# The order of the row maxima, the second batch's projections and three tiles in an attention stage

## The reference, cut to what matters

```python
qkv = hidden_states @ Wqkv
q = qkv[..., :nH * d].reshape(B, S, nH, d)
k = qkv[..., nH * d:nH * d + d]
v = qkv[..., nH * d + d:]
scores = jnp.einsum('bqhd,bkd->bhqk', q, k) * scale
...
scores = jnp.where(causal[None, None], scores + alibi[None], NEG_INF)
probs = jax.nn.softmax(scores, axis=-1)
attn = jnp.einsum('bhqk,bkd->bqhd', probs, v).reshape(B, S, H)
return attn @ Wo
```

## Time and profile before

| what | value |
|---|---|
| median of three runs | 4109.71 us |
| the profiled execution | 4106.15 us |
| its span, first to last instruction | 4104.3 us |
| TensorE busy | 3618.9 us (88%) |
| VectorE busy | 2896.3 us (71%) |
| ScalarE busy | 2364.0 us (58%) |
| mean granted TensorE clock | 0.949 of full |

### The profile page before, as it was taken

One profiled execution on the slowest core, in us unless ns is written; L12 is line 12 of the kernel. 1 busy time (PEld: TensorE's weight loads), 2 busy tenths in 40 slices (PEclk: granted clock), 3 DMA queues, 4 the chain that ended last, 5 costly groups with the idle time before them and its releaser, 6 DMA issues.

```text
span 4104.3 us, 62802 instructions
## 1 busy us (share of the span) xinstructions
PE 3618.9 (88%) x21250; PEld 1809.9 (44%) x21250; DVE 2896.3 (71%) x4627; ACT 2364.0 (58%) x4071; POOL 2065.2 (50%) x1695
## 2 busy tenths in 40 slices
PE   3889998889888779999999999989999996776799
PEld 1344443223322335555555555545555553343344
DVE  4444335773576458888888888888988886657787
ACT  4533323554456556666666766766666663446665
POOL 4600000000000337787787777778777786546754
PEclk9999997998889989999999999999999997899999
DMA  3200011001100010000000000010000001013000
GB/s 104 68 6 1 1 31 17 1 1 18 36 8 4 10 37 7 25 13 14 25 1 26 13 25 13 8 31 1 25 13 20 11 1 65 1 45 80 16 11 31
DMA packets 58879, 88.92 MB, mean 22 GB/s; under 512 B 11429, under 2 KB 32440, under 8 KB 58548
## 3 DMA queue, kind: packets, MB, share of 16 engines
q1 hardware_dynamic: 57880, 84.15, 7.3%
q10 hardware_dynamic: 672, 0.59, 0.1%
HBM read 71.05 MB, written 6.85 MB: 19 GB/s over the span
## 4 chain that ended last, share of the span: by engine, by line
PE 62%; DVE 14%; issue 8%; ACT 6%; POOL 4%; DVEq 0%; ACTq 0%; DMA 0%; POOLq 0%
PE psum L257 12%; PE psum L259 12%; PE psum L258 12%; PE psum L1388 3%; DVE arena L1550 3%; PE psum L1361 2%; PE psum L2495 2%; PE psum L2483 2%; PE psum L2491 2%; PE psum L2452 2%; PE psum L1372 2%; PE psum L3148 1%; PE psum L3149 1%; DVE x L2177 1%; PE psum L2474 1%
## 5 line engine op out<-in xcount | busy, mean ns | idle before, releaser
L257 PE MATMUL psum<-xt_hi,arena 128*128 128x512 f16 (+1 forms) x1920 | 740.5, 386 | 19.4 <-ACT arena L2005 5.9
L258 PE MATMUL psum<-xt_lo,arena 128*128 128x512 f16 (+1 forms) x1920 | 738.9, 385 | 0.0
L259 PE MATMUL psum<-xt_hi,arena 128*128 128x512 f16 (+1 forms) x1920 | 737.8, 384 | 0.0
L2278 POOL TENSOR_TENSOR arena<-arena 128x1024 f16<-128x1024 f16 x256 | 515.5, 2034 | 49.5 <-DVE arena L2089 32.4
L1501 ACT ACTIVATE arena<-psum 128x512 f32<-128x512 f32 x576 | 320.2, 598 | 276.8 <-PE psum L1372 183.4
L1550 DVE TENSOR_REDUCE arena<-psum 128x1 f32<-128x512 f32 (+3 forms) x608 | 365.3, 654 | 155.3 <-PE psum L1361 154.1
L257 PE MATMUL psum<-arena 128*128 128x512 f16 (+1 forms) x1152 | 418.0, 367 | 57.8 <-DVE arena L2913 26.6
L1306 POOL TENSOR_TENSOR rs<-sd,epsc 128x1 f32<-128x1 f32 x15 | 8.1, 540 | 819.4 <-DVE sd L1598 819.4
L258 PE MATMUL psum<-arena 128*128 128x512 f16 (+1 forms) x1152 | 417.8, 367 | 0.0
L259 PE MATMUL psum<-arena 128*128 128x512 f16 (+1 forms) x1152 | 417.7, 366 | 0.0
L2283 POOL TENSOR_TENSOR arena<-arena 128x512 f16<-128x512 f16 x256 | 314.7, 1248 | 4.8 <-PE psum L2463 4.6
(11 more groups left out here) (363 smaller groups left out, 8340.8 us busy)
## 6 DMA issues: line engine op xcount, KB each, us to landing
arena<-m_wi SPq DMA_DIRECT2D x64, 320.0 KB, 3.0
arena<-m_wo SPq DMA_DIRECT2D x32, 256.0 KB, 2.6
arena<-arena SPq DMA_DIRECT2D x90, 64.0 KB
x<-L_attn_x SPq DMA_DIRECT2D x4, 1024.0 KB, 5.3
arena<-gate_wT SPq DMA_DIRECT2D x16, 224.0 KB, 2.5
arena<-up_wT SPq DMA_DIRECT2D x16, 224.0 KB, 2.5
arena<-down_wT SPq DMA_DIRECT2D x14, 256.0 KB, 2.6
out<-x SPq DMA_DIRECT2D x3, 1024.0 KB, 4.3
```

Source lines behind the costliest of these rows:

```text
L257: nc.tensor.matmul(out, lh, rh, start=start, stop=False)
L258: nc.tensor.matmul(out, lh, rl, start=False, stop=False)
L259: return nc.tensor.matmul(out, ll, rh, start=False, stop=stop)
L2278: nc.gpsimd.tensor_tensor(m4_ar[:, q], heads[q].broadcast_to([P, HG, P]), m4_le.unsqueeze(1).broadcast_to([P, HG, P]), ALU.mult).then_inc( ...
```

## The change

It changes the plan, not the work: the ring has the same 630 entries, and the same steps run on each engine.

- The second batch's tiles come in the order 0, 3, 2, 1, 4, 5, 6, 7 (before 0, 3, 1, 4, 2, 5, 6, 7).
- The ring is made as pairs of due time and entry and sorted by due time. So projections and maxima now alternate, where before one finished before the other began.
- The projections of batch 1 start a tile sooner: the first key piece at the end of tile 5, the second and the first four query pieces at 6 units' distance in tile 6, the value piece at the start of tile 7. The other four query pieces follow at one unit's distance from the last unit of tile 7 on.
- The maxima of tiles 8, 9 and 10 are spread evenly over tile 7; those of tile 11 over the next 28 units; those of tiles 12 to 15 evenly over everything up to tile 15. Per eight score units this gives nine in tile 7 (six in its last eight), four in tile 8, then 5, 6, 9, 8 in tile 9, 9, 9, 9 in tile 10, 9, 9 in tile 11, and eight or nine from there to the end of tile 14. For tile 2 they begin before tile 0, so that tile 0 has 13 and the first eight units of tile 1 have 16.
- A row step comes as soon as three further ring entries have been placed after the last maximum, or at the latest directly before its tile. In units before the tile: rows 2 to 7 come 4 (before 6), row 8 61, rows 9 and 10 40 and 41, row 11 40, row 12 19, row 13 16, row 14 6, row 15 none.
- SyncE's loads of the weight pieces are tied to a score step 7 units before the end of a tile instead of a row step, which is where they stood; the load of the next block's weights goes with row 12 instead of row 11.

```diff
--- before.py
+++ after.py
@@ -500,7 +500,7 @@
         def row_group(half, first, n):
             return slice(half * HALF + first, half * HALF + first + n)
 
-        SEQ2 = [(0, t) for t in range(TPB)] + [(1, t) for t in (0, 3, 1, 4, 2, 5, 6, 7)]
+        SEQ2 = [(0, t) for t in range(TPB)] + [(1, t) for t in (0, 3, 2, 1, 4, 5, 6, 7)]
         POS2 = {b * TPB + t: p for p, (b, t) in enumerate(SEQ2)}
         TAIL2 = (("heads0", 1), ("o0", 2), ("heads1", 4), ("o1", 5), ("turn", 7), ("turn_hi", 8), ("turn_lo", 9),
                  ("project", 11), ("y_stats", 13), ("y_sd", 14), ("y_scale", 15), ("y_norm", 16), ("add", 17), ("x_sd", 18),
@@ -511,31 +511,31 @@
 
         def plan2():
 
-            ring, when = [], []
-
-            def feed(p, at):
-                us = max_units(SEQ2[p][1])
-                for u in range(len(us)):
-                    ring.append(("max", p, u))
-                    when.append(at(u, len(us)))
-            for piece in [("qp", 0, 0, f) for f in range(KT)] + [("kp", 0, 0), ("kp", 0, 1), ("vp", 0)]:
-                ring.append(piece)
-                when.append(-1)
-            feed(0, lambda u, n: -1)
-            for p in range(NT - 1):
-                b, t = SEQ2[p]
-                start, n = first2[p] - LEAD2, units2[p]
-                if p == TPB - 1:
-                    pieces = [("kp", 1, 0), ("kp", 1, 1)] + [("qp", 1, 0, f) for f in range(KT)] + [("vp", 1)]
-                    for i, piece in enumerate(pieces):
-                        ring.append(piece)
-                        when.append(first2[p] + 3 * i)
-                    start, n = start + n - 8, 8
-                if (b, t) in ((0, 1), (1, 3)):
-                    for f in range(KT):
-                        ring.append(("qp", b, 1, f))
-                        when.append(first2[p] + 2 * f)
-                feed(p + 1, lambda u, m: start + (u + 1) * n / m)
+            ring = []
+
+            def feed(units, start, n):
+                for i, unit in enumerate(units):
+                    ring.append((max(0, start + (i + 1) * n / len(units)), unit))
+
+            of_tile = lambda p: [("max", p, u) for u in range(len(max_units(SEQ2[p][1])))]
+            for piece in [("qp", 0, 0, f) for f in range(KT)] + [("kp", 0, 0), ("kp", 0, 1), ("vp", 0)] + of_tile(0):
+                ring.append((-1, piece))
+            for f in range(KT):
+                ring.append((first2[1] + 2 * f, ("qp", 0, 1, f)))
+            for p in range(TPB - 1):
+                feed(of_tile(p + 1), first2[p] - LEAD2, units2[p])
+            for i, piece in enumerate([("kp", 1, 0), ("kp", 1, 1)] + [("qp", 1, 0, f) for f in range(KT)]):
+                ring.append((first2[TPB - 2] + 6 * i, piece))
+            last = TPB - 1
+            ring.append((first2[last] + 3, ("vp", 1)))
+            feed(of_tile(last + 1) + of_tile(last + 2) + of_tile(last + 3), first2[last] - LEAD2, units2[last])
+            for f in range(KT):
+                ring.append((first2[last + 1] + f, ("qp", 1, 1, f)))
+            feed(of_tile(last + 4), first2[last + 1] - LEAD2, 4 * LEAD2)
+            far = [unit for p in range(last + 5, NT) for unit in of_tile(p)]
+            feed(far, first2[last + 1] + 3 * LEAD2, first2[NT - 1] - first2[last + 1] - 4 * LEAD2)
+            ring.sort(key=lambda entry: entry[0])
+            when, ring = [at for at, _ in ring], [unit for _, unit in ring]
             for r in range(len(ring) - 2, -1, -1):
                 if ring[r][0] == "max":
                     when[r] = min(when[r], when[r + 1] - 1 / 1.6 if ring[r + 1][0] == "max" else when[r])
@@ -569,7 +569,10 @@
                     while r < len(RING2) and (WHEN2[r] <= now or RING2[r] == ("max", p, RING2[r][-1])):
                         steps.append(("ring", r))
                         r += 1
-                    while rows < NT and DONE2[rows] < r and (rows <= p or now >= first2[p + 1] - LEAD2 + 1):
+                        if rows < NT and DONE2[rows] + 3 < r:
+                            steps.append(("row", rows))
+                            rows += 1
+                    if rows < NT and rows <= p:
                         steps.append(("row", rows))
                         rows += 1
                     if i == 0:
@@ -1267,12 +1270,13 @@
                         held.append(p)
                     elif piece[0] == "qp" and piece[3] == KT - 1:
                         q_rows(sp, p, piece[2], range(8) if piece[1] else range(6))
+                elif what == "score" and p + 1 >= EARLY4 and u[0] == units2[p] - LEAD2:
+                    if p + 1 < NT:
+                        if p + 1 > EARLY4:
+                            sp.wait_ge(m4_wlo, p + 1 - EARLY4 + 2)
+                        sp_piece(sp, p + 1 - EARLY4)
                 elif what == "row":
-                    if p >= EARLY4:
-                        if p > EARLY4:
-                            sp.wait_ge(m4_wlo, p - EARLY4 + 2)
-                        sp_piece(sp, p - EARLY4)
-                    if p == 11:
+                    if p == 12:
                         sp.wait_ge(a2_md, AT2["qp", 1, 1, KT - 1] + 3)
                         sp.wait_ge(a2_dma, 16 * 2 * QDMA)
                         sp.dma_start(s3_raw, A["L1_ffn_sign"].rearrange("(k p) n -> p k n", p=P)).then_inc(s3_in, 16)
```

## The result

The kernel before took 4110.86 us (median of 4 runs, 4108.85 to 4112.69) beside the changed kernel's 4067.85 (4 runs, 4064.09 to 4078.01). The ratio is 0.9899 with a 95% interval of 0.9879 to 0.9919: 1.0% less, some 43 us. The forecast was 4090 with a range from 4074 to 4112.

The account below looks back on a forecast made before the run. VectorE was taken to bound stretches full of maxima, with in-order TensorE waiting behind them. Terms -1.8, -16.8, -2.6, -2.2, -2 and +6 gave -19.4 us, from 4109.7 to 4090.3, stated as 4090, range 4074 to 4112.

Parts of the forecast that it names:

- Evenly placed maxima: In the stage's tiles, eight score units with nine evenly placed maxima should take 6 to 7 us at full clock.
- Tile 7: Tile 7 becomes like tile 6 with eight units more: 66.1 us, VectorE some 48 us busy instead of 32.5.
- merge waits: At the row transposes, TensorE's 13.7 us of waits for VectorE's merge stay, near 12 us in the profile after.
- last-maximum waits: At three other row transposes, TensorE's waits for the last maximum vanish: -2.8 us.
- the wait ahead of tile 15: Last row, directly before its tile: loses a 1.64 us maximum wait, gains a 2.26 us copy and DMA wait, net +0.6.
- level price: Tiles 8 to 14: removing 37 maxima above nine per eight units, 26 at 0.60 and 11 at 0.11 us, saves 16.8 us.
- tiles 0 and 1: Start of the stage: 14 fewer of tile 2's maxima in the burst after the projections, -2 us, bounds -8 and +5.
- clock allowance: Even stretches such as tiles 4 and 6: two more dips of the granted clock, +6 us.
- Tile 6: Tile 6 takes more projections and a 3 us wait for row copies before tile 8's first maximum: 56.8 becomes 70.2 us.
- The time only moves: Rival, 4105 us, chance 0.15: TensorE lacks room in tiles 8 to 13, so the sum is only -4.7 us.
- half clock in the even stretches: Rival, 4119 us, slower, chance 0.11: tiles 6 and 7 run partly at half clock, +34 us in place of +6.
- More than forecast: Rival, 4068 us, chance 0.06: every excess maximum costs 0.9 us (-33) and the clock dips do not come.

Follow-up runs that it names:

- lighter maxima: The kernel before, with VectorE reducing only every fourth key in tile 2's 32 maxima, nothing moved: ratio 0.9963, 4102.45 us.
- the late part alone: The changed kernel with the four query projections of the second half put ahead of tile 2's maxima again: ratio 0.9915 to the kernel before, 4079.47 us.
- the second profile: The changed kernel, unchanged, profiled and timed once more beside the kernel before: ratio 0.9891, 4068.01 us.

## Why the prediction was right in direction and wrong in size

**What held.** Evenly placed maxima do hide beneath TensorE: eight units with nine maxima take 5.7 us at 1.00 (968.0 to 973.7), under the 6 to 7 forecast and no more than eight units without any. Tile 7 was forecast at 66.1 us and took 66.1, with VectorE 44 us busy for "some 48"; tiles 8 to 13 were forecast at about 225 and took 223.0. Tile 7's hit is in part luck, since the forecast had it at full clock and it ran at 0.92. The merge waits were forecast at 12 and took 12.3 us, the last-maximum waits went, the wait ahead of tile 15 came with 2.2 us for "over 2", and that ahead of tile 8's first maximum with 4.1 for 3. The level price of 16.8 us for tiles 8 to 14 has its counterpart in the 15.3 us that taking levelness and order away together cost. But this is a number that came out, not a mechanism: I put it all on the count of excess maxima, 0.60 us each of TensorE's idle time for most of them, and the order at 0. TensorE's idle time in these tiles fell by 2.5 us only, its waits for maxima over the stage by 1.6, and level pace with the old order earned none of it.

**The step that failed: tiles 0 and 1, -2 us (bounds -8 and +5).** Up to the end of tile 2 it measured -22.5 in the profiles; in timed runs the mixing of projections and maxima gave -14 alone. I took TensorE's 96% as a sign that it had no room, and the 0.61 in the earlier trace rows as a condition that would stay. In fact the busy time was long because of the clock, and the clock was low in the burst that the change dissolves: with lighter maxima TensorE's busy time in tile 1 falls by 11.9 us with the same products, at 1.00 instead of 0.75. What comes back is the burst's VectorE time (14 fewer maxima at 0.60 are 8.4 us) and the clock; the two overlap, and no run parts them. A bound of -8 left the clock out altogether. This step is not the whole miss: the late part alone took 35 us (23 to 46), where the sum had 17.4 for all the rest.

**The sign of the clock allowance.** I added 6 us for two more dips. Half clock went down instead, by 56 to 63 us or, at 0.35, some 21 us; about half of it in tiles 0 and 1 (from 0.65 and 0.75 to 0.89 and 1.00), so this overlaps with the term above. The same mistake stands behind it: I judged dips by one profile, in which even tiles happened to be at 1.00 and 0.97, and took the dips of the uneven ones as given instead of asking what each cost. The runs show that a fuller stretch can do better ((1, 1) at 0.89 with extra products, at 0.54 to 0.72 without) and that half clock went with the wait ahead of tile 8's first maximum (4.1 us, 0.62 over the eight units around it), but tile 4, with the same instructions at 1.00 and at 0.80, shows that neither settles a single stretch.

**Tile 6.** Forecast 70.2, measured 76.5 (75.8 in the second profile). The wait was sized within 1.1 us; what was missing is the half clock around and after it, 13.6 us or, at 0.35, 4.8.

**The rivals.** "The time only moves" and "half clock in the even stretches" are refuted by ratio and by the clock, 0.92 in tile 7. "More than forecast", with a chance of 0.06 and 4068, names the measured time by another way, and that is luck: its 33 us and one projection were to come from tiles 8 to 13, which gave 24, of which tile 14 took 4 back, and as much came from ahead of tile 3.

**What stays open.** Why the order pays only with the level pace (the late rows of the old order are a part of it that was not taken apart; the changed kernel's tiles 8 to 14 save busy time and not idle time), and how much of (1, 1)'s shortening is its content and how much the clock. Why tile 4 runs at 1.00 in one execution and 0.80 in the next.

## What to carry to other kernels

A burst of VectorE work in a ring of PSUM banks that TensorE feeds in order cost twice here: VectorE's own time, and then TensorE's clock in the thin products held up by it (tile 1: VectorE 25.23 us at clock 0.75, 16.69 us at 1.00 with lighter maxima). When a stretch shows TensorE 95% busy (tile 1 had 96% at 0.75), look at its granted clock before concluding that it has no room, and take two or three profiles before a stretch's clock enters a sum. After such a change look for the waits that it made: here a 4.1 us wait went with up to 7, and moving the projections by a few units took it away. And where a sum says that waits will go, look whether TensorE's idle time did fall, and not only whether the time came out.

## What was unexpected of the hardware

- With the same instructions tile 4 took 44.2 us at clock 1.00 and 51.6 at 0.80, tile 7 71.9 at 0.98 and 83.9 at 0.78, in different executions of one order; tile 1 took 47.1 to 47.2 at 0.75 in four of them and 42.9 at 0.84 in a fifth, and 31.0 at 1.00 in both profiles of after.
- The clock was not kept up by being busy: (1, 1) had TensorE 30.38 of 33.3 us busy at 0.59, and with an extra full-size product per score it was at 0.89.
- In mixed thin products one microsecond at half clock cost about 0.35 us (an estimate from 12.0 us for 34 in tile 7 and 7.4 for 20.6 in tile 4), less than the 0.5 that would be lost if TensorE alone set the pace: in dense 128x512 products of the kernel before one starts every 0.43 us at 0.50 (1706.40 to 1709.39) and every 0.22 us at 1.00.
